# Causal maxima masked on TensorE, one scaling step moved on VectorE, and expert rows turned inside the down projection

## What is computed

```
q, k, v = heads(x @ w_qkv + b_qkv)
scores = einsum('bhid,bhjd->bhij', q, k) * attn_scale
scores = where(j >= i, scores, -inf)
attn = softmax(scores)
x = layernorm(x + (attn @ v) @ w_out + b_out)

h = relu(einsum('ceh,ehi->cei', inputs, experts_inter))
out = einsum('cei,eih->ceh', h, experts_out) * in_w[..., None]
x = layernorm(x + combined)
```

## Time and profile before

| | us |
|---|---|
| median of 3 runs | 1659.26 |
| range of these runs | 1654.88 to 1662.66 |
| the profiled execution | 1661.06 |
| its span in the trace | 1659.5 |
| layer 0, the seven full turns | about 78 to 513, some 62 each |
| layer 0, experts | 593.67 to 804 |

### The profile page before, as it was taken

How to read it: one execution, slowest core, us unless ns; L and a number is a source line. 1 busy time by engine, 2 the same in 40 slices (tenths; PEclk the granted TensorE clock), 3 DMA queues, 4 the chain that set the end, 5 groups by cost and what they waited for, 6 DMA issues and landing times.

```text
span 1659.5 us, 31170 instructions
## 1 busy us (share of the span) xinstructions
PE 1383.2 (83%) x10239; PEld 933.8 (56%) x10240; DVE 908.2 (55%) x3424; ACT 703.9 (42%) x984; POOL 495.6 (30%) x415
## 2 busy tenths in 40 slices
PE   3678898898888369999459999999998649999991
PEld 1245555555555346665325556555655448999991
DVE  1767888878886401111266766876753353434434
ACT  2145554554555111111036676767776312222223
POOL 4032344334334302122111122132312224444442
PEclk7799899999898679999779999999999769999996
DMA  6855536545513024333154647545645424444446
GB/s 168 215 107 109 116 107 133 119 111 122 120 27 116 13 71 122 107 83 83 38 113 87 121 89 149 119 93 116 133 102 148 144 85 64 71 72 71 71 63 215
DMA packets 119550, 174.71 MB, mean 105 GB/s; under 512 B 17624, under 2 KB 101618, under 8 KB 113281
## 3 DMA queue, kind: packets, MB, share of 16 engines
q1 hardware_dynamic: 96320, 148.05, 37.5%
q0 software_dynamic: 20400, 22.37, 8.6%
q10 hardware_dynamic: 2704, 2.70, 0.5%
HBM read 107.64 MB, written 72.69 MB: 109 GB/s over the span
## 4 chain that ended last, share of the span: by engine, by line
PE 55%; DVE 6%; issue 5%; ACT 4%; DMA 4%; POOL 1%; SPq 1%; POOLq 0%; DVEq 0%; ACTq 0%
PE ST L1865 7%; PE OT L769 7%; PE shared L1877 7%; PE ST L751 7%; PE ST L1324 6%; PE shared L1523 3%; PE OT L1332 3%; PE shared L1332 3%; ACT arena L890 3%; PE shared L800 3%; PE shared L1530 1%; PE shared L817 1%; DMA sum<-arena,block_to_row 1%; PE shared L781 1%; DVE scratch L1158 1%
## 5 line engine op out<-in xcount | busy, mean ns | idle before, releaser
L890 ACT ACTIVATE arena<-ST 128x1024 f32<-128x1024 f32 x416 | 412.9, 1025 | 217.9 <-PE ST L751 216.8
L751 PE MATMUL ST<-arena 96*128 96x256 bf16 (+2 forms) x1792 | 246.5, 272 | 41.8 <-DMA arena<-qk_parts 20.4
L769 PE MATMUL OT<-arena,v_aug 128*32 128x256 f32 (+1 forms) x3584 | 241.4, 384 | 5.7 <-POOL arena L1226 5.1
L751 PEld LDWEIGHTS ST<-arena 96*128 96x128 bf16 (+1 forms) x1792 | 151.0, 100 | 152.1 <-ACT arena L890 58.0
L1158 DVE CUSTOM_DVE_ANT_0 scratch<-shared,mask 128x512 bf16<-128x512 f32 (+3 forms) x293 | 135.6, 497 | 56.8 <-PE shared L865 51.8
L1972 POOL DMA_INDIRECT sum<-arena,block_to_row x71 | 111.2, 1566 | 170.9 <-DMA sum<-arena,block_to_row 118.4
L769 PEld LDWEIGHTS OT<-arena,v_aug 128*32 128x32 f32 x3584 | 92.5, 112 | 107.9 <-issue 67.4
L1877 PE MATMUL shared<-arena 128*128 x568 | 134.8, 381 | 0.0
L1226 POOL TENSOR_SCALAR_AFFINE_SELECT arena<-arena 128x512 f32<-128x512 f32 (+1 forms) x96 | 79.6, 834 | 172.2 <-ACT arena L890 172.2
L1694 POOL DMA_INDIRECT slot_x<-x_out,row_to x64 | 63.7, 995 | 165.7 <-DVE keep L1612 148.6
L1877 PEld LDWEIGHTS shared<-arena 128*128 128x128 f32 x568 | 103.0, 191 | 11.2
(11 more groups left out here) (232 smaller groups left out, 2378.8 us busy)
## 6 DMA issues: line engine op xcount, KB each, us to landing
arena<-qk_parts SPq DMA_DIRECT2D x224, 128.0 KB, 7.2
qk_parts<-qk_src SPq DMA_DIRECT2D x32, 384.0 KB, 2.6
arena<-qk_parts SPq DMA_DIRECT2D x32, 384.0 KB, 4.6
qk_parts<-qk_src SPq DMA_DIRECT2D x64, 192.0 KB, 3.0
arena<-slot_x SPq DMA_DIRECT2D x71, 130.0 KB, 2.4
arena<-qk_parts SPq DMA_DIRECT2D x32, 256.0 KB, 5.5
sum<-x_out SPq DMA_DIRECT2D x16, 512.0 KB, 3.0
arena<-in_experts_inter SPq DMA_DIRECT2D x7, 1024.0 KB, 5.1
```

The source lines that it names most:

```text
L751: mm = pe.matmul(scores[:, i * 256 + at:i * 256 + at + nq], K[par][0:rows, h, kb * P:(kb + 1) * P], Q[par][0:rows, h, q0:q0 + nq], start=T ...
L769: mm = pe.matmul(OT[32 * i:32 * i + 32, q0:q0 + nq], v_aug[par][:, kb, g * GH + i, :], PT[n % RING][:, i, at:at + nq], start=(u == 0), sto ...
L890: act.activation(PT[n % RING][:, :, :], scores[:, :].rearrange("p (h n) -> p h n", h=GH), func, scale=ATT_SCALE).then_inc(L["exp"], 1)
```

## The change

Three parts.

1. In `a_dve`, VectorE's list alone is reordered: in turns that have both, `("on", 3)`, the scaling of the last group, is done ahead of the last two fills `("mx", 38)` and `("mx", 39)`. TensorE's order stays.
2. The mask moves to TensorE. Each piece of a fill is now left open, and a further matmul per piece, identity times a bf16 tile `mask_b` of 128 columns, adds the mask onto the diagonal block in PSUM. VectorE then takes plain maxima, one `tensor_reduce` for each fill: a fill of 512 gives one maximum, 256 + 256 gives two, and 384 + 128 gives four block maxima in `mx_blocks`, which two more instructions in `mc` fold into `mx`. Reads of earlier fills that VectorE waited for are gone with the scratch output.
3. In `b_pe`, the rows of expert e + 1 are turned ahead of the last quarter (t = 3) of the down projection of expert e. ScalarE copies them as soon as they are there.

```diff
+        mask_b = sb("mask_b", [P, P], BF16)
+        mx_blocks = sb("mx_blocks", [P, NH, TB])
@@ a_pe, mx
                         for of_pair, qb, at in FILLS[n % len(FILLS)]:
                             head = n // len(FILLS) * 2 + of_pair
-                            mm = pe.matmul(bank[:, at:at + S - qb * P], Q[par][0:SK, head, qb * P:(qb + 1) * P],
-                                           K[par][0:SK, head, qb * P:S], start=True, stop=True)
+                            pe.matmul(bank[:, at:at + S - qb * P], Q[par][0:SK, head, qb * P:(qb + 1) * P],
+                                      K[par][0:SK, head, qb * P:S], start=True, stop=False, skip_group_check=True)
+
+                        for _, _, at in FILLS[n % len(FILLS)]:
+                            mm = pe.matmul(bank[:, at:at + P], ident_b[:, :], mask_b[:, :], start=False, stop=True,
+                                           skip_group_check=True)
@@ a_dve
+            def scaled_first(steps):
+                if ("on", NG - 1) in steps and ("mx", N_MX - 2) in steps:
+                    steps.remove(("on", NG - 1))
+                    steps.insert(steps.index(("mx", N_MX - 2)), ("on", NG - 1))
+                return steps
@@ a_dve, mx
-                        if n >= 2:
-                            banks.read(dve, turn, ("mx", n - 2))
-                        elif turn.kind != "first":
-                            banks.all_before_read(dve, turn)
-                        settle(dve)
-                        for of_pair, qb, at in FILLS[n % len(FILLS)]:
-                            i = (n // len(FILLS) * 2 + of_pair) * TB + qb
-                            m = S - qb * P
-                            taken = dve.tensor_tensor_reduce(
-                                out=junk[n % 2][:, at:at + m], in0=bank[:, at:at + m], in1=mask[:, 0:m],
-                                scale=1.0, scalar=LOW, op0=ALU.add, op1=ALU.max, accum_out=mx[:, i:i + 1])
-                        taken.then_inc(free, 1)
+                        if fill == 2:
+                            dve.tensor_reduce(of_all[:, head:head + 2, 2], bank[:, :].rearrange("p (h n) -> p h n", h=2),
+                                              AX_X, ALU.max).then_inc(free, 1)
+                        elif fill % 3 == 0:
+                            dve.tensor_reduce(of_all[:, head + fill // 3:head + fill // 3 + 1, 0], bank[:, :].unsqueeze(1),
+                                              AX_X, ALU.max).then_inc(free, 1)
+                        else:
+                            dve.tensor_reduce(mx_blocks[:, head + fill // 3, :],
+                                              bank[:, :].rearrange("p (b n) -> p b n", n=P),
+                                              AX_X, ALU.max).then_inc(free, 1)
@@ a_dve, mc
+                        chain.unwaited(dve.tensor_reduce(of_all[:, heads, 1], mx_blocks[:, heads, 0:3], AX_X, ALU.max))
+                        chain.step(dve.tensor_copy(of_all[:, heads, 3], mx_blocks[:, heads, 3]))
@@ b_pe
+            def turn_rows(e):
+                pe.wait_ge(b_load[e % 2], e // 2 * 48 + 48)
+                for c in range(CD):
+                    for t in range(TB):
+                        mm = pe.transpose(shared[c][:, t * P:(t + 1) * P], xg[e % 2][:, t, c * P:(c + 1) * P],
+                                          ident[:, :])
+                    mm.then_inc(b_turned, 1)
+
+            turn_rows(0)
@@ b_pe, emit, down projection
                 for t in range(TB):
+                    if t == TB - 1 and e + 1 < E0:
+                        turn_rows(e + 1)
                     for m in range(MI):
@@ b_act, emit
+                wait(act, b_up, e * MI)
                 for c in range(CD):
```

More of the change, by code:

```diff
@@ L522, in build @@
         scratch = sb("scratch", [P, S])
-        junk = [scratch[:, i * (S // 2):(i + 1) * (S // 2)].bitcast(BF16) for i in range(2)]
+        mask_b = sb("mask_b", [P, P], BF16)
         mx = sb("mx", [P, NH * TB])
+        mx_blocks = sb("mx_blocks", [P, NH, TB])
         mx_rest = sb("mx_rest", [P, NH * TB])
@@ L870, in emit @@
                         bank, ready = banks.acquire(pe, turn, ("mr", n))
-                        pe.wait_ge(L["mchain"], k * 8 + (4 * n + 4))
+                        pe.wait_ge(L["mchain"], k * 12 + (6 * n + 6))
                         settle(pe)
@@ L1122, in a_dve @@
                 dve.memset(v_aug[i][:, :, :, HD], 1.0).then_inc(s_fill, 1)
-            dve.wait_ge(s_fill, 8)
+            dve.tensor_copy(mask_b[:, :], mask[:, 0:P]).then_inc(s_fill, 1)
+            dve.wait_ge(s_fill, 9)
             dve.sem_inc(s_fill2, 1)
+            def scaled_first(steps):
[3 more added lines that the diff above has]
+                return steps
             def emit(turn):
-                for step, n in schedule(True, turn.kind):
+                for step, n in scaled_first(schedule(True, turn.kind)):
                     k, par, half = turn.batch(-1 if step in AHEAD[True] else 0)
@@ L1161, in emit @@
-                        taken.then_inc(free, 1)
-                    elif step == "mc":
-                        for i in (2, 1):
-                            banks.read(dve, turn, ("mx", (n + 1) * HALF_MX - i))
-                        chain = Chain(dve, L["mchain"], k * 8 + 4 * n)
+                        of_all = mx[:, :].rearrange("p (h b) -> p h b", b=TB)
+                        fill, head = n % len(FILLS), n // len(FILLS) * 2
+                        if fill == 2:
[8 more added lines that the diff above has]
+                                              AX_X, ALU.max).then_inc(free, 1)
+                    elif step == "mc":
+                        for b in range(banks.n):
+                            banks.read(dve, turn, ("mx", max(i for i in range(n * HALF_MX, (n + 1) * HALF_MX)
+                                                             if banks.place[turn.kind][("mx", i)][0] == b)))
+                        chain = Chain(dve, L["mchain"], k * 12 + 6 * n)
+                        heads = slice(n * HH, (n + 1) * HH)
+                        of_all = mx[:, :].rearrange("p (h b) -> p h b", b=TB)
+                        chain.unwaited(dve.tensor_reduce(of_all[:, heads, 1], mx_blocks[:, heads, 0:3], AX_X, ALU.max))
+                        chain.step(dve.tensor_copy(of_all[:, heads, 3], mx_blocks[:, heads, 3]))
@@ L1309, in b_pe, with emit @@
             pe.wait_ge(LA["oe"], NB * NG)
-            def emit(e, par, half):
-                pe.wait_ge(b_load[par], half * 48 + 48)
-                wait(pe, b_turned_out, e * CD)
+            def turn_rows(e):
+                pe.wait_ge(b_load[e % 2], e // 2 * 48 + 48)
                 for c in range(CD):
                     for t in range(TB):
-                        mm = pe.transpose(shared[c][:, t * P:(t + 1) * P], xg[par][:, t, c * P:(c + 1) * P],
+                        mm = pe.transpose(shared[c][:, t * P:(t + 1) * P], xg[e % 2][:, t, c * P:(c + 1) * P],
                                           ident[:, :])
                     mm.then_inc(b_turned, 1)
+            turn_rows(0)
+            def emit(e, par, half):
                 pe.wait_ge(b_turned_out, e * CD + CD)
```

## The result

| | before | after |
|---|---|---|
| median of 13 runs each, us | 1659.86 | 1665.78 |
| lowest to highest | 1654.88 to 1665.03 | 1656.23 to 1670.56 |
| the profiled execution | 1661.06 | 1656.23 |
| its span | 1659.5 | 1654.7 |

The ratio is 1.0036, 95% interval [1.0021, 1.0051]: the change costs 6 us. The sign is the one forecast, the size less than half of the 13.7 us. Run again later on two chips, the same kernel gave 1.0054 [1.0034, 1.0075] (`e5_change`) and 1.0028 [1.0014, 1.0042] (`g1_change`). Mind the table: the profiled execution of after is the fastest of its 13. Its span read alone would say "faster".

What follows compares the result with a forecast made beforehand. TensorE was taken to bound the long middle of a turn, waiting for VectorE at its end. Terms: 7 x 2.4 = 17, + 1, - 4.4 = +13.6 us, for a median of 1673 us, range 1655 to 1686.

Steps and rivals of the forecast that it cites:

- The sign: Whole kernel: the change was forecast to make it slower, by +13.6 us in the sum.
- The price of one: Mask matmul on TensorE: 56 ns each at full clock, taken as 66 ns on average.
- the share that is hidden: Mask matmuls on TensorE: 27 of 64 a turn fall into time in which it would wait anyhow.
- 37 x 66 ns = 2.4 us a turn: TensorE in the turns: the 37 mask matmuls not hidden in waits lengthen each turn by 2.4 us.
- The clock case: Rival, turns: shorter waits give TensorE full clock for a third of its half-speed time, 12 us gained, 1661; chance 0.15.
- VectorE's relief: VectorE in the turns: plain maxima save net 1.1 us of 50 a turn, but `ps` comes only 0.15 us earlier.
- The first part in sum: Masks on TensorE: 7 x 2.4 = 17 us in full turns and +1 us in the first turn.
- The scaling: End of a turn: scaling ahead of fills 38 and 39 lets TensorE start `oT` earlier, -0.2 us.
- VectorE would stand for 0.25: End of a turn: VectorE, ready at about 385.80, waits 0.25 us for TensorE to write the last group.
- scaling in front stalls: Rival, end of a turn: VectorE stands at the last group while two filled banks wait, +7 us, 1680; chance 0.10.
- Experts: Between experts: 0.74 us of TensorE idle time goes, six times, a gain of 4.4 us.

Runs made afterwards that it cites:

- e5_change: The change as it is, all three parts, run again beside other kernels on one chip: 1.0054 of before.
- e6_zeros: The kernel before, masks still on VectorE, with 512 added TensorE matmuls of a tile of zeros: 1.0024 of before.
- f2_no_scale: The change without its second part (scaling at its old place, behind the last fills), run again on one chip: 0.9961 of before.
- f3_nomask: The change without its second part and without the mask matmuls, so masked keys enter the maxima: 0.9883 of before.
- e3_scale: The kernel before with the second part alone, scaling ahead of fills 38 and 39, masks on VectorE: 1.0030 of before.
- e2_masks: The kernel before with the first part alone, mask matmuls on TensorE and plain maxima on VectorE: 0.9998 of before.
- e7_zeros3: The kernel before, masks still on VectorE, with 1536 added TensorE matmuls of a tile of zeros: 1.0187 of before.
- f1_relief: The kernel before with plain maxima on VectorE alone, no mask on the maxima and no mask matmuls: 0.9957 of before.

## Where the prediction was right and where it was wrong

**Masks.** The price of one was right (56 ns apart at full clock: the two masks at 195.44 in after start within 0.11 us), and the share that is hidden nearly so (1.5 us a turn for 1.8). Wrong was the term "37 x 66 ns = 2.4 us a turn", what the uncovered ones cost. I took it as added in full, 17 in all. Measured are 4 on before (`e6_zeros`, 1 to 7) and 13 on a kernel whose VectorE is relieved (`f2_no_scale` against `f3_nomask`, 6 to 20, which does not exclude 17). Why the two differ stays open, if they do. The clock case, which I had as a rival at 0.15, is in part true: busy time rose by 10 us (`g2_no_scale`) where 21.5 were issued, and on one chip the executions of `e6_zeros` had 31 us less at 1.2 GHz than those of before. I had noted the rival and left it out of the sum. A small slip lies in the 66 ns too: 17% of the time at half speed is only 9% of the matmuls, which makes 56 / 0.915 = 61 ns on average and 1.3 us less of the 17. The rule of the Trainium skill that I had quoted, "TensorE: Matmul & The Clock Gate", section "Back-to-back issue gap", with 81 ns a pair, is not borne out: 55 to 60 ns in the traces, less in the sum.

**VectorE's relief.** Each duration was right: a plain maximum of 512 columns takes 0.68 us, 0.61 apart; VectorE is busy 322.17 less 313.79 = 8.4 us less in the six turns with maxima of that stretch, 1.4 a turn against 1.1. But I gave its way to `ps` and `oT` only 0.15 us and set 0.35 against it for `mc` and `mr`. Measured are 7 us (3 to 12), some 1 us a turn. `ps` to `oT` holds 2.5 of this. In the other 55 us of a turn the waits for VectorE seemed to have no weight; where its relief counts there stays open. On the way to `ps` it is in part lost again: the four products in front of `ps` take 0.75 us longer in five of six turns in the kernels with plain maxima (last section), which the forecast does not have.

**The first part in sum** was forecast at 18 us slower with the first turn, and measured at 0, give or take 3 (0.9998, and 0.9953 against 0.9955 with the experts, on one chip): too much for the masks, by 5 to 14 us as one takes the one pair or the other, and some 7 too little for the relief.

**The scaling** was forecast at -0.2 us a turn, within an end of turn that I took as unchanged, and it costs 13 us in the change (5 on before, 2 to 8 with the noise; VectorE stands 9.4 us in six turns of `e3_scale` and 12.4 in `g1_change`). The step that failed is "VectorE would stand for 0.25". It was read from one turn of before in which the stretch behind `ps` had the full clock, and it is right for such turns (0.32). In the others the last group comes 1.6 us later (4.9 against 3.26 us after `ps`), and VectorE, which does not slow down with TensorE, stands 1.8 us and more: 1.78, 1.78 and 2.91 in after, 1.8 to 2.9 in `g1_change`. Five of the six turns of before were of this kind. The rival "scaling in front stalls" named this mechanism and its margin; I gave it 1 us a turn and a chance of 0.10. It was the main thing that happened: without it the change would be 0.995.

**Experts.** 6.1 us in the traces instead of 4.4, 7.5 by the ratio, whose interval takes in both; the term counted the idle time and not the transposes' tail.

**The sum.** Forecast +13.7: take off 18 for the first part, add 13 for the scaling, take off 3 for the experts, and it is +6, which is what was measured. Each of these numbers is uncertain by 3 us or more, so that they meet this well is chance. The right sign was luck: two errors that cancel for the most part, 18 us too many for the first part and 13 too few for the second.

**A faster version.** `g2_no_scale`, the change without its second part, beats both kernels with the computation as it was, 0.9948 of before. `f3_nomask` goes further, to 0.988 (0.984 on another chip), by leaving the mask out of the maxima. The softmax divides by its own sum, so a larger number subtracted cancels; but scores whose masked neighbours are far larger would underflow. That is argued, and wasn't tried with such data.

## What to carry to other kernels

Before a step is put ahead of others on an engine that works in order, compare when its input comes with when the engine arrives, in every turn and at the producer's slower clock, not in one turn: here the engine stood 0.3 us at 2.4 GHz and 1.8 us at 1.2 GHz. Work that is ready belongs ahead of work that may be late; one fill of 0.6 us and three small steps in between made a loss of 0.8% into one of 0.2%. And where a part both loads one engine and relieves another, measure the two halves apart: here a relief of some 7 us met a load of 4 to 13, and their sum was zero.

## What the runs showed of the hardware

PEclk differs between executions of the same program with the same instructions: over the stretch of seven turns 0.94 in after and 0.90 in `g1_change`, on one chip 0.899 to 0.911 over the whole span in 31 executions of before (1678.98 to 1693.68 us). The turn from the first `oT` to the second took 61.70 us in after, at 0.97, and 64.40 in `g1_change`, at 0.90; 1.7 of the difference lie between `ps` and `oT`:

```profile
143.20:204.90 61.70, 55.68 (x527) 37.37 (x527) 48.98 (x132) 32.03 (x42) 16.87 (x17) 0.97 0.48 96
```
```profile
143.10:207.50 64.40, 59.09 (x527) 39.16 (x527) 48.93 (x132) 31.61 (x41) 16.88 (x17) 0.90 0.47 99
```

So one trace of each kernel can't settle a difference of 10 us here; the medians did.

The four products at `r_before`, the last instructions of VectorE in front of `ps`, took 0.92 to 0.94 us in before, in five of its six turns, and 1.68 or 1.69 in as many turns of every kernel with plain maxima (but for one of 1.53 in `e2_masks`). In the sixth turn it was 2.23 against 1.71 to 1.89. The rows show a coincidence that is the same each time. One of the four takes as long as a GpSimd instruction of 1.10 us beside it still runs, and they end together: the first of them in before, for 0.33 us, the third in after, for 1.10. The others take 0.16. In `e7_zeros3`, where no GpSimd instruction ran beside them, the four took 0.75. First before, then after:

```profile
380.11 1.10 POOL L1226 TENSOR_SCALAR_AFFINE_SELECT arena<-arena 128x1024 f32<-128x1024 f32 x1 [1.33 <-ACT arena L890]
380.88 0.93 DVE L1044 TENSOR_TENSOR r_before<-r_before,r_mask 128x8 bf16<-128x8 bf16 x4
```
```profile
383.57 1.68 DVE L1049 TENSOR_TENSOR r_before<-r_before,r_mask 128x8 bf16<-128x8 bf16 x4
383.94 1.10 POOL L1245 TENSOR_SCALAR_AFFINE_SELECT arena<-arena 128x1024 f32<-128x1024 f32 x1 [1.56 <-ACT arena L895]
```

So plain maxima brought the products to a place where they take longer, 0.75 us a turn on the way to `ps`. No run moved the GpSimd instruction, so that it is the cause is not shown, but the two ended together in each of the first five turns of before, after, `f1_relief` and `g2_no_scale`.
